# Two transformer layers on one core: the second layer's opening in another order, and the first layer's last store on another queue

## What is computed

```python
x = x + norm(attn(norm(x)))          # 16 sequences, 16 heads of 8 features, 256 keys each
x = x + norm(ffn(norm(x)))
# ffn: the first axis is now the sequence (16 long), the 256 tokens are the batch
y = layer_norm(x + mha(x), g1, be1)  # 4 heads of 32 features, 16 keys each
idx = argmax(y @ Wg.T)               # one of 8 experts for each token
out = relu(y @ W1[idx] + b1[idx]) @ W2[idx] + b2[idx]
return layer_norm(y + out, g2, be2)
```

## Time and profile before

| what | value |
|---|---|
| median of 3 runs | 702.21 us (701.7 to 703.17) |
| the profiled execution's own time | 709.53 us |
| span of its profile (first to last instruction) | 707.8 us |
| mean granted TensorE clock | 0.887 of full |
| instructions | 16656 |

### The profile page before, as it was taken

How to read it: one execution, slowest core, us unless ns; L and a number is a source line. 1 busy time by engine, 2 the same in 40 slices (tenths; PEclk the granted TensorE clock), 3 DMA queues, 4 the chain that set the end, 5 groups by cost and what they waited for, 6 DMA issues and landing times. The chain is left out here.

```text
span 707.8 us, 16656 instructions
## 1 busy us (share of the span) xinstructions
PE 583.3 (82%) x5511; PEld 432.4 (61%) x5511; DVE 429.0 (61%) x1212; ACT 376.7 (53%) x989; POOL 305.2 (43%) x535
## 2 busy tenths in 40 slices
PE   4999999999999999999980789888869208999920
PEld 3565666666666666666540677777766208999910
DVE  2454667666666666666422488877895612788870
ACT  1014665565566565565550498778861004677760
POOL 5311133323332233312126327777768730076676
PEclk9558999999999999999795699999997557999975
DMA  5000000000000000000015500000001112134333
GB/s 152 12 2 2 3 2 17 18 16 3 18 17 17 18 17 18 18 15 5 18 31 156 149 3 1 2 2 0 0 18 39 51 63 68 37 53 66 32 33 32
DMA packets 28592, 21.60 MB, mean 31 GB/s; under 512 B 3513, under 2 KB 26849, under 8 KB 28514
## 3 DMA queue, kind: packets, MB, share of 16 engines
q1 hardware_dynamic: 21330, 15.42, 8.6%
q0 software_dynamic: 6640, 4.92, 4.9%
q10 hardware_dynamic: 544, 0.26, 0.1%
HBM read 10.11 MB, written 8.12 MB: 26 GB/s over the span
## 5 line engine op out<-in xcount | busy, mean ns | idle before, releaser
L383 DVE TENSOR_REDUCE nmax<-psA 128x2 f32<-128x512 f32 x256 | 165.2, 687 | 122.7 <-PE psA L206 122.5
L511 ACT ACTIVATE pr<-psB 128x512 f32<-128x512 f32 x250 | 135.8, 595 | 126.0 <-PE psB L223 124.4
L206 PE MATMUL psA<-km,q 24*128 24x256 f32 x768 | 139.9, 428 | 3.9 <-POOL km L603 2.5
L223 PE MATMUL psB<-q,km 26*128 26x256 f32 (+1 forms) x752 | 111.2, 417 | 0.0
L206 PEld LDWEIGHTS psA<-km,q 24*128 24x128 f32 x768 | 92.0, 198 | 29.9 <-issue 18.1
L1604 POOL DMA_INDIRECT out<-wz,ys x39 | 61.4, 1573 | 60.1 <-ACT wz L1569 53.4
L603 POOL TENSOR_TENSOR km<-kraw,rows_of 128x768 f32<-128x768 f32 x16 | 23.5, 1466 | 119.0 <-DVEq L362 115.2
L237 PE MATMUL psO<-pr,v 128*32 128x256 f32 x1024 | 71.1, 397 | 1.3 <-ACT osb L505 1.1
L223 PEld LDWEIGHTS psB<-q,km 26*128 26x128 f32 (+1 forms) x752 | 69.9, 193 | 0.4 <-issue 0.3
L577 POOL TENSOR_SCALAR ve<-mv_r 128x2 f32<-128x2 f32 x16 | 3.7, 231 | 128.3 <-DVE mv_r L344 128.3
L1473 DVE TENSOR_TENSOR hT<-psH,e_nb1T 128x512 f32<-128x512 f32 x39 | 27.0, 691 | 41.6 <-PE psH L1434 32.5
(11 more groups left out here) (203 smaller groups left out, 1225.8 us busy)
## 6 DMA issues: line engine op xcount, KB each, us to landing
ys<-y_sorted SPq DMA_DIRECT2D x39, 72.0 KB, 1.8
xs<-x_all SPq DMA_DIRECT2D x16, 128.0 KB
out<-x_all SPq DMA_DIRECT2D x16, 128.0 KB, 3.7
e_w<-W SPq DMA_DIRECT2D x1, 2048.0 KB
e_w<-W SPq DMA_DIRECT2D x4, 512.0 KB
x_all<-x SPq DMA_DIRECT2D x1, 1536.0 KB, 10.3
q<-mT SPq DMA_DIRECT2D x64, 4.0 KB
out<-wz,ys POOLq DMA_INDIRECT x39
```

Source lines behind the costliest of these rows:

```text
L206: last = T.matmul(psA[:, n % 2, c * L1:(c + 1) * L1], queries(b, h, depth, slice(c * P, (c + 1) * P)), keys(b, h, depth, slice(0, L1)), st ...
L223: last = T.matmul(bank_of(b, h)[:, c * L1:(c + 1) * L1], keys(b, h, depth, slice(c * P, (c + 1) * P)), queries(b, h, depth, slice(0, L1)), ...
L383: V.tensor_reduce(nmax[:, b % 2, :, h], psA[:, n % 2, :].rearrange("p (c m) -> p c m", c=2), AX.X, ALU.max, negate=True).then_inc(S["a_fre ...
L511: A.activation(pr[:, h % PRING, :, :].rearrange("p c l -> p (c l)"), bank_of(b, h), ACT.Exp, scale=SCALE1).then_inc(S["b_free"], 1)
```

## The change

Four things are done. The store of the last sequence of layer one is issued by ScalarE, behind a wait for `x1_ok`, in place of SyncE's `x1_out(LAST)`. In the second block VectorE goes straight to the statistics of the first pair; the mask is made behind them and ahead of `apply_x(0)`, and TensorE waits for it where the scores begin. The copies to uT and wgT go from VectorE to ScalarE, as its first instructions, and ScalarE's wait for `q_zero` moves to where it writes qT2. GpSimd's constants become three functions, called behind `add_bo` in iterations 1, 2 and 3, and the memset of qT2 stands between the first `ready_x` and the first `add_bo`.

```diff
--- before.py
+++ after.py
@@ -551,6 +551,9 @@
             max_rows(0, 0)
             for i in range(LAST + 3):
                 iteration(i)
+            act.wait_ge(S["x1_ok"], B1)
+            act.dma_start(out[LAST * L1:B1 * L1, :].rearrange("(p c) d -> p c d", p=P),
+                          x_all[:, 2 * LAST:2 * B1, :]).then_inc(kept, 16)


         @block.gpsimd
@@ -695,7 +698,6 @@
             for i in range(LAST + 3):
                 iteration(i)
             x1_over(LAST)
-            x1_out(LAST)
             sp.wait_ge(S["stored"], 16 * B1)
             sp.wait_ge(kept, 16 * B1)

@@ -836,7 +838,6 @@
             last = T.transpose(psS[1][:, 0:NE], wg_nat[:, :], ident[0:NE, 0:NE])
             last.then_inc(S["wT_full"], 1)
             pe.wait_ge(S["wT_ok"], 2)
-            pe.wait_ge(S["mask_ok"], 1)

             def sums(k):

@@ -874,6 +875,7 @@
                     last.then_inc(S["vo_full"], 1)
                 if has(t, 2):
                     i, n = t - 2, (m - 2) % 2
+                    pe.wait_ge(S["mask_ok"], 1)
                     pe.wait_ge(S["q_ok"], count(i + 1))
                     pe.wait_ge(S["k_ok"], count(i + 1))
                     for c in range(2):
@@ -947,16 +949,16 @@
         def _(dve):
             V = nc.vector

-            V.tensor_reduce(same[:, :], ident[:, :].rearrange("p (s r) -> p r s", r=8), AX.X,
-                            ALU.add).then_inc(S["same_ok"], 1)
-            dve.wait_ge(S["same_ok"], 1)
-            V.tensor_scalar(mask[:, :].rearrange("p (s r) -> p s r", r=8),
-                            same[:, :].unsqueeze(1).broadcast_to([P, S2, 8]), -1.0, 1e30, ALU.add,
-                            ALU.mult).then_inc(S["mask_ok"], 1)
-            dve.wait_ge(S["wT_full"], 1)
-            V.tensor_copy(uT[:, :, :].rearrange("p k d -> p (k d)"), psS[0][:, :]).then_inc(S["wT_ok"], 1)
-            V.tensor_copy(wgT[:, :], psS[1][:, 0:NE]).then_inc(S["wT_ok"], 1)
             dve.wait_ge(loaded2, 16 * len(loads2))
+
+            def make_mask():
+
+                V.tensor_reduce(same[:, :], ident[:, :].rearrange("p (s r) -> p r s", r=8), AX.X,
+                                ALU.add).then_inc(S["same_ok"], 1)
+                dve.wait_ge(S["same_ok"], 1)
+                V.tensor_scalar(mask[:, :].rearrange("p (s r) -> p s r", r=8),
+                                same[:, :].unsqueeze(1).broadcast_to([P, S2, 8]), -1.0, 1e30, ALU.add,
+                                ALU.mult).then_inc(S["mask_ok"], 1)

             def norm_x(i, n):

@@ -1056,6 +1058,8 @@
                     mark(SORT_AT[t])
                 if has(t, 0):
                     norm_x(t, m % 2)
+                if isinstance(t, int) and t == 0:
+                    make_mask()
                 if has(t, 1):
                     dve.wait_ge(S["qk_full"], count(t))
                     dve.wait_ge(S["s_full"], count(2 * (t - 1) - 2))
@@ -1169,7 +1173,9 @@
         def _(act):
             A = nc.scalar
             act.wait_ge(loaded2, 16 * len(loads2))
-            act.wait_ge(S["q_zero"], 1)
+            act.wait_ge(S["wT_full"], 1)
+            A.activation(uT[:, :, :].rearrange("p k d -> p (k d)"), psS[0][:, :], ACT.Copy).then_inc(S["wT_ok"], 1)
+            A.activation(wgT[:, :], psS[1][:, 0:NE], ACT.Copy).then_inc(S["wT_ok"], 1)

             def exponentials(i, n, c):
                 act.wait_ge(S["max_ok"], count(2 * i + c + 1))
@@ -1181,6 +1187,7 @@

             def iteration(t, m):
                 if has(t, 1):
+                    act.wait_ge(S["q_zero"], 1)
                     act.wait_ge(S["qk_full"], count(t))
                     act.wait_ge(S["s_full"], count(2 * (t - 1) - 2))
                     act.wait_ge(S["k_ok"], count(t))
@@ -1229,29 +1236,34 @@
         @block.gpsimd
         def _(pool):
             G = nc.gpsimd
-            G.memset(zeros[:, :, :], 0.0).then_inc(S["ids_ok"], 1)
-            pool.wait_ge(S["ids_ok"], 1)
-            G.iota(zeros[:, :, P:P + 1].bitcast(I32), [[1, NPAD]], base=B1 * L1, channel_multiplier=NPAD
-                   ).then_inc(S["zeros_ok"], 1)
-            G.memset(y_all[:, :, P:], 0.0)
-            G.memset(w["b2p"][:, :], 0.0)
-            G.memset(w["top"][:, :], 0.0).then_inc(S["ids_ok"], 1)
-            pool.wait_ge(S["ids_ok"], 2)
-            G.memset(w["top"][0:1, :], 1.0).then_inc(S["ids_ok"], 1)
-            G.iota(y_all[:, :, P:P + 1].bitcast(I32), [[1, NT]], base=0, channel_multiplier=NT
-                   ).then_inc(S["ids_ok"], 1)
-            pool.wait_ge(S["ids_ok"], 4)
-            for e in range(NE):
-                G.memset(pref[:, e:e + 1], float(NE - e))
-                G.memset(base[:, e:e + 1], float(e * REGION))
-            for k in range(2):
-                G.memset(run[k][:, 0:CHUNK // 2, :], 0.0)
-            G.memset(every[:, :], 1.0).then_inc(S["consts"], 1)
-            pool.wait_ge(S["consts"], 1)
-            G.affine_select(out=before[:, :], in_=every[:, :], compare_op=ALU.is_gt, fill=0.0, base=0,
-                            pattern=[[1, P]], channel_multiplier=-1).then_inc(S["consts"], 1)
-            G.memset(qT2[:, :, :, :], 0.0).then_inc(S["q_zero"], 1)
             pool.wait_ge(loaded2, 16 * len(loads2))
+
+            def blank_rows():
+                G.memset(zeros[:, :, :], 0.0).then_inc(S["ids_ok"], 1)
+                pool.wait_ge(S["ids_ok"], 1)
+                G.iota(zeros[:, :, P:P + 1].bitcast(I32), [[1, NPAD]], base=B1 * L1, channel_multiplier=NPAD
+                       ).then_inc(S["zeros_ok"], 1)
+
+            def token_numbers():
+                G.memset(y_all[:, :, P:], 0.0)
+                G.memset(w["b2p"][:, :], 0.0)
+                G.memset(w["top"][:, :], 0.0).then_inc(S["ids_ok"], 1)
+                pool.wait_ge(S["ids_ok"], 2)
+                G.memset(w["top"][0:1, :], 1.0).then_inc(S["ids_ok"], 1)
+                G.iota(y_all[:, :, P:P + 1].bitcast(I32), [[1, NT]], base=0, channel_multiplier=NT
+                       ).then_inc(S["ids_ok"], 1)
+                pool.wait_ge(S["ids_ok"], 4)
+
+            def sort_constants():
+                for e in range(NE):
+                    G.memset(pref[:, e:e + 1], float(NE - e))
+                    G.memset(base[:, e:e + 1], float(e * REGION))
+                for k in range(2):
+                    G.memset(run[k][:, 0:CHUNK // 2, :], 0.0)
+                G.memset(every[:, :], 1.0).then_inc(S["consts"], 1)
+                pool.wait_ge(S["consts"], 1)
+                G.affine_select(out=before[:, :], in_=every[:, :], compare_op=ALU.is_gt, fill=0.0, base=0,
+                                pattern=[[1, P]], channel_multiplier=-1).then_inc(S["consts"], 1)

             def scale_of(agg, step, i, mv, ve, nm, rs):

@@ -1292,8 +1304,12 @@
             def iteration(t, m):
                 if has(t, 0):
                     ready_x(t, m % 2)
+                if isinstance(t, int) and t == 0:
+                    G.memset(qT2[:, :, :, :], 0.0).then_inc(S["q_zero"], 1)
                 if has(t, 0):
                     add_bo(t, m % 2)
+                if isinstance(t, int) and 1 <= t <= 3:
+                    (blank_rows, token_numbers, sort_constants)[t - 1]()
                 if isinstance(t, int) and t == 17:
                     for k in range(40):
                         G.memset(number[:, k:k + 1], float(k))
```

## The result

The change makes the kernel faster: 700.41 us in the median of 22 executions (697.7 to 707.2) against 703.61 of 22 executions of the kernel before. The ratio is 0.9933, with a 95 % interval of 0.9912 to 0.9955, which is 3.2 to 6.2 us of 703.61, with 4.7 in the middle. The forecast was 4.5. The two medians taken by themselves lie 3.2 apart, at the lower end of that. The forecast time of 697.7 was worked out from 702.21 for the kernel before; the measured ratio makes 697.5 of 702.21.

A forecast was written before the change was run, and what follows sets the result against it. The prediction took TensorE, standing still at the seam for the first x2n behind GpSimd's constants, as the bound. Terms 0.5 + 4.3 − 0.1 − 0.2 = 4.5 us, from 702.21 to 697.7; range 695.2 to 700.0.

The forecast's parts named there:

- The store: Seam of the layers: ScalarE issues the last store 0.65 us earlier, beside the copy to xs; gain 0.5, bounds 0 and 0.65.
- x2n held: Opening of layer two: qT2's memset holds the first x2n until about 4.2 us after the opening; gain 4.3; chance 0.52.
- The rival that x2n is not held: Opening: x2n runs free of qT2's memset, starting at 2.4; gain 6.3 us in all, time 695.9; chance 0.28.
- The argument against the hold: First x2n: kT's 484 ns and x2n's 343 give the same fixed part, 202 ns, so no sign of a faster mode.
- The mask: Opening, on VectorE between statistics and x2n: fits inside the 1.55 us wait for the scale; 0.1 lost, bounds 0 and 0.3.
- The weight copies: Opening, on ScalarE from about 1.4 us: through by 2.8, before TensorE wants them, so they hide.
- The constants: Iterations 1 to 3 on GpSimd: blocks lie in idle time or under cover; contention costs 0.2 us, bounds 0 and 1.2.
- scales of iterations 2 to 4 ahead of their x2n: Sign of success in layer two's first iterations: GpSimd's scales are ready before the x2n that uses them.
- a sign of being wrong: Layer two's iterations: the prediction is wrong if GpSimd's blocks end up in front of a waiting VectorE.
- TensorE's clock rises at its old hour: Rival, first iterations: work arriving 4.8 us earlier runs at half rate, 2.4 is given back, time 700.1; chance 0.10.
- the gain at x2n to be found again at the first load of ys: Check late in layer two: the prediction is wrong if x2n's gain is not found again at the first ys load.

The follow-up runs named there:

- clear_split: The kernel after with qT2 cleared in two halves, the first at once, the second behind the first bias addition; 696.75 us, ratio 0.9913 to the kernel before.
- constants_first: The kernel after with GpSimd again writing all its constants and qT2's memset ahead of the first scale; 702.58 us, ratio 0.9989 to the kernel before.
- opening_only: The kernel after with the last store back on SyncE's queue behind the copy to xs; 700.41 us, ratio 0.9917 to the kernel before.
- fill_after: The kernel after with TensorE products nobody reads added at layer one's end and in the opening; 694.81 us, ratio 0.9855 to the kernel before.

## Why the prediction was right, and where its terms were off

**The store, 0.5 forecast, 0.17 measured: mis-sized.** The step that failed took the store as what SyncE waits for last, since the earlier trace rows shows only it. The copy to xs had a wait of its own hidden behind it: landing 4.2 after its issue, as here, it lands in before at 376.63 + 4.2 = 380.8, 0.2 ahead of the store's 377.28 + 0.46 + 3.3 = 381.0. So no more than 0.2 was to be had. The prediction noted that the copy has no landing in the trace, but let that lower only the size it took, not the bound.

**x2n held, 4.3 forecast, 4.78 measured: the mechanism was right, the size a little low.** The scale came at +2.40, as worked out, and the memset held x2n. clear_split shows it: without a memset beside it x2n runs at its own length and ends 1.25 earlier. What the sum had wrong is the end: it let x2n begin when the memset ended and then run its 0.60, while the held pieces end within 0.14 of the memset. The mask in the earlier trace rows had ended 0.08 behind a memset in the same way, so the row was there. The rival that x2n is not held is out.

The Trainium skill (SBUF — State Buffer, "SBUF: two separate sides") makes VectorE and GpSimd block each other for whole instructions where VectorE uses both pairs of ports. The 1793 ns beside a memset of 1.81 us agree with it; the runs show the hold, not the ports. The argument against the hold, that x2n's rate shows no faster mode, was no guide.

**The mask, 0.1 forecast, 0 measured.** It took 0.23 where GpSimd does small work only, 0.76 in constants_first and 1.51 in before, beside memsets. It was through 1.0 before the scale.

**The weight copies** on ScalarE were done at 378.57, +2.05, ahead of anything that wants them: hidden, as forecast.

**The constants, 0.2 forecast: hidden in the profiled pair, in part on the path where the clock is up.** The product and its neighbour on GpSimd do meet, as expected: prob took 1.24, as in the earlier trace rows, and the last constant 0.73 in place of 0.29. But x2n doesn't move by it. Behind blank rows the third scale was ready 0.19 ahead of its x2n, just the margin worked out (399.40 and 399.59); the sign "scales of iterations 2 to 4 ahead of their x2n" held for the second and the third, and the fourth waited 0.86 for its scale, as it did before the change (0.85). But that margin was read from a stretch at the lower clock. In opening_only and fill_after, where the clock rose ahead of the third x2n, that x2n waited 0.70 and 0.71 behind the blank rows. There GpSimd's block stood in front of a waiting VectorE, which the prediction had named as a sign of being wrong. By the fourth x2n little of that is left: 4.57 of the 4.79 in the pair with added products.

**The clock: a rival came true in part.** "TensorE's clock rises at its old hour" had 0.10 and a price of 2.4. The prediction let the clock rise about 11 after the first x2n starts, as it did in before (19.5 − 8.48). In the kernel after it rose 14.3 after it (16.7 − 2.44), and 0.9 was given back by the fourth x2n. In opening_only it rose earlier than in either. The step that failed is the reading that the clock follows the scores; what decides it is open. These are single executions, so the 0.9 is no fixed term of the change.

**Sum.** 0.17 + 4.78 − 0.9 is about 4.0 at the fourth x2n in the profiled pair; the runs give 4.7 (3.2 to 6.2). The forecast of 4.5 was right in part because the store's 0.3 too much and x2n's 0.5 too little cancel. The prediction asked for the gain at x2n to be found again at the first load of ys. It is found only in part in this pair: that load starts 201.9 after the opening in before (583.4) and 198.8 here (575.3), 3.1 earlier, with 4.31 still there at the last x2n and 2.60 at the end of the span (326.28 and 323.68). What takes the difference between the last x2n and that load was not tried and stays open; single executions differ there by up to 3.5 us (76.9 in fill_after, 80.4 in the kernel after). That the gain reaches the time is shown by the runs' ratio alone.

## What to carry to other kernels

Where a stage opens, put first what the long chain waits for, and follow that chain over all engines: the wait here sat in GpSimd's constants, and moving VectorE's work alone gave nothing. Beside a memset of GpSimd count a VectorE operation such as x2n or the mask as ending just behind the memset, not as starting there. Work that is hidden behind TensorE's products at the lower clock can stand in the way at the upper one: the margin of 0.19 was gone in opening_only and fill_after, where the clock rose ahead of the third x2n. Where several transfers end a stage, the row shows only the last; work out the landing of the second before crediting the first's removal.

## What was not expected of the hardware

- The rise of TensorE's granted clock differs between executions that give TensorE the same products in the same order up to there: 16.7 after the opening in the kernel after, 9.4 in opening_only, and the fourth x2n moves by 2.9 us with it. The stretch from 346 to 357 is at 0.53 in before, at 0.54 in opening_only and at 1.00 in the kernel after. With products that nobody reads the clock was at 1.00 from 370 on through the first iterations, and the gap from first to fourth x2n shrank by 3.1 us in the kernel before.
- A copy of 128 KB inside the on-chip memory landed 4.2 us after its issue, later than a store of the same size from ScalarE's queue (1.7) or SyncE's (3.7).
